# Shared experts of a mixture-of-experts layer: weights as the stationary operand and 512 tokens moving, biases as columns, one product for the combination, and the spreading of token rows set apart

## What is computed

```
x = x + layernorm(attention(layernorm(x)))
x = x + layernorm(experts(layernorm(x)))

def expert(x, g, gb, w1, b1, w2, b2):          # g, w1: 512 x 256; w2: 256 x 512
    y = gelu(x @ g + gb) * (x @ w1 + b1)
    return y @ w2 + b2

aff = sigmoid(x @ wa); p, i = top_k(aff, 2)    # 16 routed experts, 2 of them for each token
combine[token, i] = p / sum(p)
routed = sum over e of combine[token, e] * expert_e(x)
shared = expert_0(x) + expert_1(x)             # 2 shared experts, all tokens
experts(x) = x + shared + routed
```

## Time and profile before

| what | value |
|---|---|
| median of three runs | 2145.7 us |
| profiled execution | 2147.81 us, its span 2146.1 us |
| mean granted TensorE clock | 0.888 |
| PE / weight loads / VectorE / ScalarE / POOL busy, share of the span | 83% / 48% / 41% / 27% / 22% |
| shared stage, first to last product | 1147.80 to 1546.54 us |
| routed stage, first to last product | 1562.26 to 2068.6 us |

### The profile page before, as it was taken

One profiled execution on the slowest core, in us unless ns is written; L12 is line 12 of the kernel. 1 busy time (PEld: TensorE's weight loads), 2 busy tenths in 40 slices (PEclk: granted clock), 3 DMA queues, 4 the chain that ended last, 5 costly groups with the idle time before them and its releaser, 6 DMA issues.

```text
span 2146.1 us, 24008 instructions
## 1 busy us (share of the span) xinstructions
PE 1788.8 (83%) x7806; PEld 1035.7 (48%) x7807; DVE 885.6 (41%) x2047; ACT 581.2 (27%) x1151; POOL 466.4 (22%) x653
## 2 busy tenths in 40 slices
PE   4488888888888888887656999999889999999950
PEld 3254555545555454554344566666544444444420
DVE  2544546464554646455433421121222323223238
ACT  2133334242333434234422111111112222222203
POOL 1012122222212222122110211111112222222237
PEclk8688888898898989889767999999989999999985
DMA  3434354553445454243222444444356675655558
GB/s 113 60 74 82 73 128 94 119 129 67 118 92 128 94 119 109 52 122 98 109 89 72 162 148 153 153 154 150 129 153 166 187 192 133 159 136 128 113 151 354
DMA packets 117410, 271.46 MB, mean 126 GB/s; under 512 B 15228, under 2 KB 40830, under 8 KB 110408
## 3 DMA queue, kind: packets, MB, share of 16 engines
q1 hardware_dynamic: 100792, 232.30, 37.6%
q0 software_dynamic: 16496, 37.63, 9.2%
HBM read 248.50 MB, written 109.34 MB: 167 GB/s over the span
## 4 chain that ended last, share of the span: by engine, by line
PE 69%; DVE 10%; issue 7%; ACT 5%; DMA 4%; POOL 3%; SPq 1%; POOLq 0%; DVEq 0%; ACTq 0%
PE bank L1766 26%; PE bank L1975 10%; PE bank L1992 5%; PE bank L1870 4%; PE bank L1847 4%; PE bank L1873 3%; PE bank L1830 3%; DVE tmp L1241 2%; PE bank L1965 1%; PE bank L1957 1%; PE bank L1979 1%; ACT P L1059 1%; PE bank L1953 1%; PE bank L1933 1%; DVE rp L1249 1%
## 5 line engine op out<-in xcount | busy, mean ns | idle before, releaser
L1309 DVE TENSOR_REDUCE mx<-bank 128x1 f32<-128x512 f32 (+3 forms) x352 | 219.7, 635 | 209.6 <-PE bank L1832 208.8
L1059 ACT ACTIVATE P<-bank 128x512 f32<-128x512 f32 x320 | 190.5, 595 | 411.6 <-PE bank L1847 410.8
L1975 PE MATMUL bank<-ring,xg 128*128 x632 | 286.9, 597 | 0.0
L1830 PE MATMUL bank<-Ks,Qs 96*128 96x384 f32 (+3 forms) x512 | 168.9, 397 | 68.0 <-DVE mx L1309 36.4
L1766 PE MATMUL bank<-ws,xt 128*128 128x512 f32 x768 | 196.6, 405 | 12.7 <-DMA xt<-xt_scratch 12.7
L1847 PE MATMUL bank<-Qs,Ks 97*128 97x512 f32 x320 | 162.8, 509 | 41.6 <-ACT P L1059 35.8
L1766 PEld LDWEIGHTS bank<-ws,xt 128*128 128x128 f32 x768 | 141.4, 191 | 73.2 <-issue 31.4
L1975 PEld LDWEIGHTS bank<-ring,xg 128*128 128x128 f32 x632 | 114.9, 192 | 115.6 <-issue 115.6
L1830 PEld LDWEIGHTS bank<-Ks,Qs 96*128 96x128 f32 x512 | 109.4, 231 | 109.4 <-DVE mx L1309 51.3
L1766 PE MATMUL bank<-wo_s,ynr 128*128 128x512 f32 x384 | 131.6, 469 | 35.4 <-DVE x L1368 23.9
L1673 POOL TENSOR_SCALAR_AFFINE_SELECT P<-P 128x256 f32<-128x256 f32 (+1 forms) x192 | 92.9, 486 | 302.9 <-ACT P L1059 302.8
(11 more groups left out here) (232 smaller groups left out, 2615.6 us busy)
## 6 DMA issues: line engine op xcount, KB each, us to landing
ring<-in_w SPq DMA_DIRECT2D x79, 1024.0 KB
ring<-in_w SPq DMA_DIRECT2D x79, 512.0 KB
Qs<-st SPq DMA_DIRECT2D x192, 128.0 KB, 4.6
xs<-xs_scratch SPq DMA_DIRECT2D x79, 258.0 KB, 3.8
xs_scratch<-xs_scratch SPq DMA_DIRECT2D x78, 258.0 KB, 5.0
xt<-xt_scratch SPq DMA_DIRECT2D x32, 512.0 KB, 3.3
xs<-xn_scratch SPq DMA_DIRECT2D x64, 256.0 KB, 2.9
xt_scratch<-xt SPq DMA_DIRECT2D x30, 512.0 KB, 4.9
```

Source lines behind the costliest of these rows:

```text
L1059: e.activation(Pt[:, p, :], bank[PA.bank[step]][:, :], ACT.Exp, scale=SCALE).then_inc(s_exp, 1)
L1309: e.tensor_reduce(mx[:, G % 2, :].rearrange("p (h i) -> p h i", i=4)[:, h:h + n, i:i + 1], bank[PA.bank["max", b, p, j]][:, 0:n * k].rearr ...
L1830: e.matmul(ps[:, o * k:o * k + k], Qs[0:96, 4 * g + h + o, i * 128:(i + 1) * 128], Ks[0:96, b % 2, g, 0:k], start=o == 0, stop=False)
L1975: e.matmul(ps[:, :].rearrange("p (o n) -> p o n", o=1), xg[:, q, 128 * k:128 * k + 128], ring[:, bass.ds(reg[n], 1), 512 * k:512 * k + 512 ...
```

## The change

The up products have the weights as the stationary operand (128 x 128) and the tokens as the moving one: 512 tokens of four tiles, in four pieces of 128. A unit is now a group of four tiles, one expert and one half of its 256 columns; its 24 products fill a pair of PSUM banks, one for the gate and one for the other factor. There are 32 units. The result has the hidden features on the partitions, so it needs no transposition, and the biases are columns: one is the bias operand of ScalarE's gelu, the other is added by VectorE in the same operation that multiplies. A tile's down step makes both experts' 12 products at once, four rounds after the unit with its number. The last biases, of the shared and of the routed experts, come from one product of 80 rows: `comb3` holds the high parts of the weights of combination twice and the low parts once, with ones for the shared experts, and `b2_s` the high parts of the biases, the low parts and the high parts again. Tokens are loaded by groups of four tiles; `xt` and `hT` lie where `x1s` is loaded later.

The step `spread` no longer follows `down` and is handed out at 1.25 per round from the step 8 of the router on; VectorE's row copy and SP's next load of rows are in that step. After the last spread step SP fetches the rows of four routed blocks and the weights of three. The first routed steps wait for the whole shared stage (`"shared"` in the list of banks). The router's two products use other banks. Semaphores, and the operands of the routed steps, are renamed to fit.

```diff
-    GU, TR, OU = Banks(0, 3), Banks(3, 2), Banks(5, 3)
-    N = SH * NT
+    PAIRS, TR, OU = Banks(0, 2), Banks(7, 1), Banks(4, 3)
+    N = 2 * SH * NT // 4
...
     def shared():
-        for n in range(N + 2):
+        for n in range(N + 4):
             if n < N:
                 s = P.add("up", n)
-                GU.done(P.on(GU, s))
-            if 0 <= n - 1 < N:
-                s = P.add("turn", n - 1)
+                PAIRS.done(P.on(PAIRS, s))
+            if n >= 4:
+                s = P.add("cT", n - 4)
                 TR.done(P.on(TR, s))
-            if 0 <= n - 2 < N:
-                m = n - 2
-                if m % SH == 0:
-                    s = P.add("cT", m // SH)
-                    TR.done(P.on(TR, s))
-                    P.on(OU, ("down", m), ("out", m // SH))
-                else:
-                    P.bank["down", m] = P.bank["down", m - 1]
-                P.add("down", m)
-                if m % SH == SH - 1:
-                    OU.done(P.bank["down", m])
+                s = P.add("down", n - 4)
+                OU.done(P.on(OU, s))
             yield
 
     def spread():
         for t in range(NT):
-            while ("down", SH * t + SH - 1) not in P.nth or ("route", 8) not in P.nth:
+            while ("route", 8) not in P.nth:
                 yield
             P.add("spread", t)
             yield
 
     route = router()
     next(route)
-    interleave((route, 1), (shared(), 1), (spread(), 1))
+    interleave((route, 1), (shared(), 1), (spread(), 1.25))
+    GU, TR, OU = Banks(0, 3), Banks(3, 2), Banks(5, 3)
+    for banks in (GU, TR, OU):
+        banks.had = ["shared"] * banks.n
...
+            at = here() - NT * 2048
+            xt = nc.alloc_sbuf_tensor_at("xt", [128, 2, 4, 1024], F32R, offset=at)
+            hT = nc.alloc_sbuf_tensor_at("hT", [128, 2, 4, 2, 512], F32R, offset=at + 2 * 16384)
...
+            comb3 = sb2("comb3", [128, NT, 80], F32R)
+            b1_s = sb2("b1_s", [128, SH, 4])
+            b2_s = sb2("b2_s", [80, 512], F32R)
...
+            elif was == "shared":
+                w.wait_ge(h_dve, 4 * NG)
+                w.wait_ge(cT_act, NT)
+                w.wait_ge(zs_dve, NT)
...
+        def unit(n):
+
+            return n // 4, n % 4 // 2, n % 2
...
-            bw = wst[0:2, 0:1024]
-            for x_ in range(SH):
-                if x_:
-                    w.wait_ge(b_act, 3 * x_)
-                e.dma_start(bw[:, 0:512], b1[x_]).then_inc(d_b, 16)
-                e.dma_start(bw[:, 512:1024], b2[x_]).then_inc(d_b, 16)
-            w.wait_ge(b_act, 3 * SH)
+            e.dma_start(b1_s[:, :, :].rearrange("p a b -> p (a b)"), b1c).then_inc(d_b, 16)
+            e.dma_start(wst[0:80, 512:1024], b2k).then_inc(d_b, 16)
             e.dma_start(wst[0:48, 0:512], rb).then_inc(d_b, 16)
-            e.dma_start(b2r[:, :], b2[SH:SH + E, 0, :]).then_inc(d_b, 16)
-
-            def load(t):
-                if t < NT:
-                    if t >= 2:
-                        w.wait_ge(up_pe, SH * (t - 1))
-                    e.dma_start(xt[:, t % 2, :].bitcast(F32), XT[t]).then_inc(d_xt[t % 2], 16)
+
+            def load(g):
+                if g < NG:
+                    if g >= 2:
+                        w.wait_ge(up_pe, 4 * (g - 1))
+                    for i in range(4):
+                        e.dma_start(xt[:, g % 2, i, :].bitcast(F32), XT[4 * g + i]).then_inc(d_xt[g % 2], 16)
 
             def load_rows(t):
                 if t < NT:
                     s = t % 2
                     if t >= 2:
                         w.wait_ge(d_sc[s], 32 * (t // 2))
-                        w.wait_ge(zs_dve, t - 1)
                     for n in range(2):
                         e.dma_start(xs[:, s, n, 0:512], rows_of(XN, t)).then_inc(d_xs[s], 16)
 
@@ -912,8 +910,6 @@
                 if j < NS:
                     s = j % 4
                     if j < 4:
-                        w.wait_ge(down_pe, SH * NT)
-                        w.wait_ge(zs_dve, NT)
...
                     if j >= NSLOT:
                         w.wait_ge(rdown_pe, j - NSLOT + 1)
                     elif j >= 3:
-                        w.wait_ge(down_pe, SH * NT)
+                        w.wait_ge(down_pe, NT)
...
-                if kind == "up" and n % SH == SH - 1:
-                    load(n // SH + 2)
+                if kind == "up" and n % 4 == 3:
+                    load(n // 4 + 2)
                 elif kind == "spread":
+                    load_rows(n + 2)
+                    if n == NT - 1:
+                        for j in range(4):
+                            fetch_rows(j)
+                            if j < 3:
+                                fetch_w(j)
...
+            w.wait_ge(d_b, 48)
+            e.activation(b2_s[:, :], wst[0:80, 512:1024], ACT.Copy).then_inc(b_act, 1)
             e.activation(rb_s[:, :], wst[0:48, 0:512], ACT.Copy).then_inc(b_act, 1)
-            w.wait_ge(b_dve, SH + 1)
-            e.activation(rb_s[32:48, :], wst[32:48, 512:1024], ACT.Copy).then_inc(b_act, 1)
+            w.wait_ge(comb_dve, 2)
+            for c in (0, 32):
+                e.activation(comb3[:, :, c:c + E], comb[:, :, :], ACT.Copy).then_inc(comb_act, 1)
...
                 if kind == "up":
+                    g, x_, f = unit(n)
                     w.wait_ge(up_pe, n + 1)
                     if n >= 2:
                         w.wait_ge(h_dve, n - 1)
-                    e.activation(gl[:, n % 2, :], bank[PM.bank[step]][:, 0:256], ACT.Gelu).then_inc(gl_act, 1)
-                elif kind == "turn":
-                    w.wait_ge(turn_pe, n + 1)
-                    if n >= 2:
-                        w.wait_ge(down_pe, n - 1)
-                    e.activation(hT[:, n % 2, 0, :], bank[PM.bank[step]][:, 0:256], ACT.Copy).then_inc(hT_hi, 1)
+                    e.activation(gl[:, n % 2, :], bank[2 * PM.bank[step]][:, :], ACT.Gelu, bias=b1_s[:, x_, f:f + 1]).then_inc(gl_act, 1)
+                    w.wait_ge(h_dve, n + 1)
+                    if g >= 2:
+                        w.wait_ge(down_pe, 4 * (g - 1))
+                    e.activation(hT[:, g % 2, n % 4, 0, :], hb[:, n % 2, :], ACT.Copy).then_inc(hT_hi, 1)
...
+            e.memset(comb3[:, :, :].bitcast(F32), 0.0).then_inc(comb_dve, 1)
...
+            w.wait_ge(b_act, 1)
+            e.tensor_tensor(b2_s[32:64, :], wst[32:64, 512:1024], b2_s[32:64, :], ALU.subtract).then_inc(b_dve, 1)
+            w.wait_ge(b_act, 2)
+            e.tensor_tensor(rb_s[32:48, :], wst[32:48, 0:512], rb_s[32:48, :], ALU.subtract).then_inc(b_dve, 1)
+            w.wait_ge(comb_dve, 1)
+            for c in (E, 32 + E):
+                e.memset(comb3[:, :, c:c + SH].bitcast(F32), 1.0).then_inc(comb_lo, 1)
+            w.wait_ge(comb_act, 1)
+            e.tensor_tensor(comb3[:, :, 64:64 + E], comb[:, :, :], comb3[:, :, 0:E], ALU.subtract).then_inc(comb_lo, 1)
...
                 elif kind == "up":
+                    g, x_, f = unit(n)
                     w.wait_ge(gl_act, n + 1)
                     if n >= 2:
-                        w.wait_ge(turn_pe, n - 1)
-                    e.tensor_tensor(hb[:, n % 2, :], bank[PM.bank[step]][:, 256:512], gl[:, n % 2, :], ALU.mult).then_inc(h_dve, 1)
-                elif kind == "turn":
+                        w.wait_ge(hT_hi, n - 1)
+                        w.wait_ge(hT_lo, n - 1)
+                    e.scalar_tensor_tensor(hb[:, n % 2, :], bank[2 * PM.bank[step] + 1][:, :], b1_s[:, x_, 2 + f:3 + f], gl[:, n % 2, :],
+                                           ALU.add, ALU.mult).then_inc(h_dve, 1)
                     w.wait_ge(hT_hi, n + 1)
-                    e.tensor_tensor(hT[:, n % 2, 1, :], bank[PM.bank[step]][:, 0:256], hT[:, n % 2, 0, :], ALU.subtract).then_inc(hT_lo, 1)
-                elif kind == "down" and n % SH == SH - 1:
-                    t, s = n // SH, (n // SH) % 2
+                    e.tensor_tensor(hT[:, g % 2, n % 4, 1, :], hb[:, n % 2, :], hT[:, g % 2, n % 4, 0, :], ALU.subtract).then_inc(hT_lo, 1)
+                elif kind == "down":
+                    t = n
                     w.wait_ge(down_pe, n + 1)
-                    w.wait_ge(d_xs[s], 32 * (t // 2 + 1))
                     if t >= 3:
                         w.wait_ge(d_zs[t % 3], 16 * (t // 3 + 2 * (t % 3 == 0)))
                     e.tensor_copy(zs[:, t % 3, :], bank[PM.bank[step]][:, :]).then_inc(zs_dve, 1)
+                elif kind == "spread":
...
-                    t, x_ = divmod(n, SH)
-                    s, ps = t % 2, bank[PM.bank[step]]
-                    w.wait_ge(d_xt[s], 16 * (t // 2 + 1))
-                    w.wait_ge(b_act, 3 * SH)
+                    g, x_, f = unit(n)
+                    w.wait_ge(d_xt[g % 2], 64 * (g // 2 + 1))
                     moe_bank_free(w, step)
-                    products(ps[:, :], 4, lambda a_, k: xt[:, s, 512 * a_ + 128 * k:512 * a_ + 128 * k + 128],
```

(39 more changed lines are left out.)

100 lines of the change are left out of this document (44 added, 56 removed).

## The result

Four runs of the changed kernel took 2015.39 to 2019.77 us, median 2016.35; four of the kernel before, beside them, 2142.91 to 2152.19, median 2147.3. The ratio is 0.9392 (95% interval 0.9368 to 0.9417): faster by 6.1%. The prediction was 2029 us, with a range of 2008 to 2062. The profiled execution took 2016.81 us, 131.0 less than the profiled one of before, where the sum said 117.0.

A forecast was written before the change was run, and what follows sets the result against it. It took PE (TensorE) to bound the shared and routed stages. Start 1140.0, stage end 1436.3 and first routed product 1445.3 instead of 1562.26 gave 117.0 us less: 2030.8 profiled, 2029 us for the median, range 2008 to 2062.

The forecast's parts named there:

- PE per tile: Shared stage: bias products, transpositions and f32 combination go, one 0.43 us product replaces them; 9.24 us a round against 12.13.
- Three pauses of 0.43 us a round: Shared rounds: seams at transposition and combination, taken as 0.43 each; -19 us if all vanish, +17 if the first costs 0.95.
- change of kind: PE switching between kinds of product: about 0.2 us on top, on either side of a bias product.
- The rest of the stage: Shared stage: four up-only rounds of 5.54 us, four without up of 3.50, cold start 1.4; stage 296.3 us.
- What hides the rest: ScalarE and VectorE in shared rounds: about 1.5 and 2.4 of 9.24 us; the combination's copy ready with 0.6 us slack.
- Rival 2: Shared stage: gelu, product or latencies take 1.5 us longer, combination waits 0.9 us in 28 rounds; 25 us, 2054; 13 in 100.
- Spreading: Row load, copy and scatter at 1.25 tiles a round: 7.9 us a turn, under a 9.24 round; costed at nothing.
- Head: Before the first up product: tokens issued at 1132.5, PE begins at 1140.0, 7.8 us earlier; bounds 1139 and 1148.
- rival 3: Head and seam give nothing (tokens land evenly; Z's store holds the first transposition to the end): 2044; 5 in 100.
- Seam: Last shared to first routed product: 9.0 us instead of 15.72, gain 6.7; bounds 4 and 15.7.
- Four pieces: Up products' moving tokens read in four pieces of 128: taken to cost nothing.
- Rival 4: Four pieces drop the 768 up products to plain f32 pace, 0.43 each: +153 us, 2182; 3 in 100.

The follow-up runs named there:

- the contiguous run: Kernel after, with the up products' tokens read as one run of 512 instead of four pieces of 128 (other numbers, same amount): 2017.39 us, ratio 0.9371.

## Why the prediction was right, and where it was off

- **PE per tile.** Right: bias products, transpositions and the f32 combination go, and PE stays the bound (VectorE is not at a quarter or less in both stages, as the prediction reads the earlier trace rows: in the routed one it is at 29%). The up products were spaced by 0.227 to 0.23 us for a predicted 0.231.
- **Three pauses of 0.43 us a round: the step that was mis-sized.** The prediction took them from the bias products of the earlier trace rows, as the price of a change of kind. There is none: 24 ups 5.50 for 5.74, transposition 0.02 for 0.10, downs 2.83 for 2.97, combination 0.24 for 0.43. That is 0.65 us in each of 28 rounds, 18 us. The pause belongs to products of at most 64 rows, and the new combination has 80. The prediction had named this case, -19 us if all three vanish, and took the nearest row instead. With 48 rows the kernel takes 2028.56 us: near the forecast, for part of its reason only, since its pauses (0.39 a round) are smaller than the 0.65 assumed; that the rest cancels is luck.
- **The rest of the stage.** Rounds with one half only were 5.44 for 5.54 and 3.11 for 3.50 (2 us together). Against that, the start at the lower clock lasted longer than in the earlier trace rows: the first 120 products took 30.1 us for 27.2 at full clock, 2.9 instead of 1.4, and the one wait of 0.9 cost 1.1. The 2.9 belong to this execution: its granted clock was 0.50 until 1148, and in those of nine other kernels with this stage the 120 products took 28.6 to 29.6 us. So -18.2 - 2.0 + 1.5 + 1.1 = -17.6: 278.7 for 296.3.
- **What hides the rest.** Right but for one round. The copy of the combination's weights was to be ready 0.6 us early; it ended 0.35 early (1174.79, the product at 1175.14), since the downs ahead of it took less time than forecast. Rival 2 did not come, but it was near. The prediction had no PE wait on this copy, and one came: it put only the unit's product behind a waiting row copy, and left out the router's operations, which stood there too.
- **Spreading.** Right: covered at 1.25 a round (the row copies waited once in four rounds, as forecast), and shown not to be at 2. Why the stall of the earlier trace rows went was argued, and no run tests it. The Trainium skill, "DMA: Bandwidth & Descriptors", "Issuing engines are not separate DMA queues", lets all issuers' transfers interleave on the same engines; the load of rows lands in a median of 2.9 us in the kernel after and 3.6 at two a round, which fits; these medians do not tell POOL's scatters from SP's own loads of tokens.
- **Head.** 9.22 us for 8.83, so 7.4 us gained of 7.8; in the profiled executions of eight kernels with the same head and attention it was 9.4 to 10.2. If the tokens behind had shared the engines evenly PE would have begun 8 us later; that half of rival 3 is refuted. The Trainium skill, "DMA: Bandwidth & Descriptors", "Queues, rings and completion order", has the descriptors of one queue taken in ring order on each engine. The trace agrees: PE began 7.9 us after the first load of tokens was issued, with 3.1 MB issued behind the first group.
- **Seam.** The chain was right link by link: with E the end of round 31 (1408.3), the first fetch was issued at E + 7.9 (7.8 predicted) and the stores at E + 18.8 (18.7). But VectorE went on 3.3 us after that store's issue, for 2.0; the store's median in the kernel after is 3.4, and the DMA share of the window is 0.72, which fits, but no run took the fetched weights away alone. The first routed product came at E + 24.9 for 23.0. And the four last rounds were 1.4 us shorter, so PE stood longer: 12.3 us for 9.0. It gave 3.4 of a forecast 6.7; the reordered fetches gave 6.8 more. The first routed group took 4.45 us, where 6.19 had been carried over from the earlier trace rows.
- **Four pieces.** Right, shown by the contiguous run. Rival 4's price was misread: "eight" in the earlier trace rows are eight records of four plain f32 products, so that pace is 0.86 each and not 0.43, 0.63 us more than an F32R product, and 768 of them would have cost some 480 us and not 153.

The 14.0 us between the sum and the run are these: +20.2 from the rounds, -1.5 and -1.1 from the start at the lower clock and the stall, -3.3 at the seam, -0.4 at the head, -1.8 in attention, +2.0 in the routed stage and the tail, together 14.1.

## What to carry to other kernels

Before a pause between two kinds of instructions is carried over to new code, look which property of the rows it goes with: here it was the number of rows of the narrow product, and padding bias products from 2 or 48 rows to 80 with zeros took 8 and 24 us off a kernel for a few lines each (and 30 off the kernel before). A step taken out of a stage (the spreading) frees its end only if what the next stage needs is not queued in front of what the old one still waits for; interleave the two in one queue by due time. Work that repeats with the rounds is covered until its turn (here some 8 us of load, copy and scatter) is longer than the time that the plan gives it, and what else stands behind it on the same engine counts too.

## What the runs showed of the hardware that was not expected

- An F32R product of 2, 48 or 64 rows and 512 columns holds PE for 0.42 to 0.43 us and delays its neighbours by some 0.1 to 0.2 us each, where one of 80 rows takes 0.23 to 0.24, as one of 128 does. One of 16 rows in plain f32 takes 0.95 to 1.05, where 0.86 is the rule.
- Among plain f32 products an F32R product of 48 rows costs 0.34 us more a block than one of 80 (6.38 and 6.04).
- A plain f32 product of 512 columns costs 0.86 us among its like (two records of 0.43) and 0.83 among F32R products, for 0.24 in F32R.
- A moving operand in four pieces of 128 costs as much as one run of 512 (5.50 and 5.49 us for 24).
